# The normalised rows of layer 2 go out already split: one ACT copy less per tile, stores and loads of both parts in place of a plain copy

## The reference, cut to what matters

```python
x = layernorm(x + attn_1(x))                      # layer 1
# layer 2
a = attention(rmsnorm(x, ln1_w))                  # 16 heads of 32, causal
mod = 0.1 * tanh(a @ A)
h = rmsnorm(x, ln2_w)
gate = silu(h @ W_in.T + mod * (h @ A) @ B)
up = h @ W_up.T
x = layernorm(x + x + (gate * up) @ W_down.T)
```

## Time and profile before

| | before |
|---|---|
| time, median of 3 runs | 2830.97 us (2830.84 to 2834.05) |
| the profiled execution, its own time | 2830.6 us |
| its span in the profile | 2828.7 us |
| mean granted TensorE clock | 0.973 of full speed |
| busy: PE, DVE, ACT, POOL | 93%, 56%, 47%, 23% |
| SP's queue (q1): packets, MB, share of the 16 DMA engines | 170676, 260.57, 38.3% |

### The profile page before, as it was taken

How to read it: one execution, slowest core, us unless ns; L and a number is a source line. 1 busy time by engine, 2 the same in 40 slices (tenths; PEclk the granted TensorE clock), 3 DMA queues, 4 the chain that set the end, 5 groups by cost and what they waited for, 6 DMA issues and landing times.

```text
span 2828.7 us, 40920 instructions
## 1 busy us (share of the span) xinstructions
PE 2642.4 (93%) x13584; PEld 2020.4 (71%) x13584; DVE 1580.3 (56%) x4310; ACT 1334.4 (47%) x2755; POOL 645.5 (23%) x527
## 2 busy tenths in 40 slices
PE   5999999999768999999999989999999999999998
PEld 4777777777446666666666656888888888888886
DVE  4778777777635877787786775222222333333333
ACT  2777777777624666666666665111111321111111
POOL 5466655556321222212212211000000000000000
PEclk8999999999868999999999989999999999999999
DMA  5566656665535545546545544111111311111100
GB/s 137 103 149 144 137 124 140 145 147 132 132 98 130 121 102 136 120 105 134 119 107 132 114 103 143 64 55 46 46 46 47 102 58 47 46 46 46 46 30 30
DMA packets 173802, 276.44 MB, mean 98 GB/s; under 512 B 29108, under 2 KB 53428, under 8 KB 172980
## 3 DMA queue, kind: packets, MB, share of 16 engines
q1 hardware_dynamic: 170676, 260.57, 38.3%
q0 software_dynamic: 2304, 12.58, 1.3%
q10 hardware_dynamic: 640, 1.05, 0.1%
HBM read 97.03 MB, written 42.99 MB: 50 GB/s over the span
## 4 chain that ended last, share of the span: by engine, by line
PE 53%; DVE 7%; SPq 3%; issue 3%; ACT 3%; DMA 2%; POOL 0%; ACTq 0%; DVEq 0%; POOLq 0%
PE b_scores_ps L2428 13%; PE b_lin_ps L2417 13%; PE b_pv_ps L2398 6%; PE b_scores_t_ps L2398 6%; PE b_lin_ps L1955 5%; PE b_pv_ps L307 2%; DVE b_prob L290 2%; PE b_lin_ps L1918 2%; PE b_scores_t_ps L271 2%; DVE b_junk L202 1%; PE b_scores_ps L188 1%; DMA b_k_stack<-b_k_split 1%; SPq L258 1%; SPq L254 1%; PE b_lin_ps L2423 1%
## 5 line engine op out<-in xcount | busy, mean ns | idle before, releaser
L290 DVE TENSOR_TENSOR a_prob<-a_scores_t_ps,a_prob 128x384 fp32r<-128x384 f32 (+1 forms) x384 | 225.4, 593 | 135.0 <-ACT a_scores_t_ps L283 133.5
L282 ACT ACTIVATE b_prob<-b_scores_t_ps 128x384 fp32r<-128x384 f32 (+1 forms) x384 | 199.7, 520 | 212.5 <-PE b_scores_t_ps L273 191.3
L290 DVE TENSOR_TENSOR b_prob<-b_scores_t_ps,b_prob 128x384 fp32r<-128x384 f32 (+1 forms) x384 | 226.8, 594 | 118.1 <-ACT b_scores_t_ps L283 117.4
L307 PE MATMUL a_pv_ps<-a_prob,a_value 128*65 128x512 f32 (+3 forms) x1024 | 272.3, 334 | 0.5 <-DVE a_prob L290 0.5
L282 ACT ACTIVATE a_prob<-a_scores_t_ps 128x384 fp32r<-128x384 f32 (+1 forms) x384 | 201.9, 526 | 148.9 <-PE a_scores_t_ps L273 124.2
L307 PE MATMUL b_pv_ps<-b_prob,b_value 128*33 128x512 f32 (+3 forms) x1024 | 270.6, 333 | 0.1
L202 DVE CUSTOM_DVE_ANT_0 b_junk<-b_scores_ps,spare 128x512 bf16<-128x512 f32 (+3 forms) x512 | 226.9, 483 | 61.5 <-PE b_scores_ps L188 60.2
L202 DVE CUSTOM_DVE_ANT_0 a_junk<-a_scores_ps,spare 128x512 bf16<-128x512 f32 (+3 forms) x512 | 226.9, 483 | 34.4 <-PE a_scores_ps L188 32.2
L2365 DVE TENSOR_TENSOR b_res<-b_scores_ps,b_first_gate 128x512 f32<-128x512 f32 x64 | 44.2, 691 | 333.5 <-PE b_scores_ps L2428 333.5
L2365 DVE TENSOR_TENSOR stage<-b_scores_ps,b_junk 128x512 f32<-128x512 f32 x64 | 44.3, 692 | 329.0 <-PE b_scores_ps L2428 329.0
L990 PE MATMUL a_lin_ps<-x_split,w_split 128*128 128x512 f32 x768 | 215.5, 398 | 0.0
(11 more groups left out here) (298 smaller groups left out, 5874.3 us busy)
## 6 DMA issues: line engine op xcount, KB each, us to landing
a_q_stack<-a_q_split SPq DMA_DIRECT2D x192, 128.0 KB, 3.5
a_k_stack<-a_k_split SPq DMA_DIRECT2D x192, 128.0 KB, 3.6
b_q_stack<-b_q_split SPq DMA_DIRECT2D x192, 128.0 KB, 3.3
b_k_stack<-b_k_split SPq DMA_DIRECT2D x192, 128.0 KB, 3.7
spare<-h_t SPq DMA_DIRECT2D x16, 1024.0 KB, 6.2
stage<-in_x_t SPq DMA_DIRECT2D x8, 1024.0 KB, 6.7
a_sum_hi<-a_pv_raw SPq DMA_DIRECT2D x32, 256.0 KB, 3.8
spare<-a_pv_raw SPq DMA_DIRECT2D x32, 256.0 KB, 4.0
```

The lines of the kernel that those rows point to most:

```text
L282: act.activation(at.prob_hi[:, k % at.ring, 0:w], at.scores_t_ps[:, k % 2, 0:w], ACT.Exp, scale=SCALE)
L290: dve.tensor_tensor(at.prob_lo[:, k % at.ring, 0:w], at.scores_t_ps[:, k % 2, 0:w], at.prob_hi[:, k % at.ring, 0:w], ALU.subtract).then_in ...
L307: mm = pe.matmul(at.pv_ps[0:at.vcols, h % 2, kt * P:SEQ], at.value[:, kt, g * GH + h, :], prob[:, k % at.ring, col:col + width], start=(kt ...
```

## The change

The plain copy h_turn is gone. ACT makes only the high part of each tile; DVE takes the low part from the PSUM bank itself. The DRAM tensor h_t now holds both parts, 2 MB a batch in place of 1, and `store_h` stores them from h_split in two transfers of 1 MB once all four tiles are split; in step g=2 it now stands after spread_in instead of ahead of spread_out. The MLP loads both parts straight into its operand tiles (`load_h`, two transfers of 1 MB), and `input_hi` and `input_lo` are gone. As DVE now reads the bank, PE's transposes of tiles 2 and 3 wait for h_split_ready instead of h_hi, and the first projections for it too. The load for run 0 moves from step g=3 of the last batch to its step g=2, ahead of gather.

```diff
-            def store_h(b, t):
-                apart(sp, at.ones_set, h_copied, b * TT + t + 1)
-                sp.dma_start(h_hbm[:, :, bass.ds(b * SEQ + t * P, P)], h_turn[:, t, :, :]).then_inc(h_out, 16)
+            def store_h(b):
+                sp.wait_ge(h_split_ready, (b + 1) * TT)
+                for part in range(2):
+                    sp.dma_start(h_hbm[part, :, :, bass.ds(b * SEQ, SEQ)],
+                                 h_split[:, part, :, :].bitcast(F32)).then_inc(h_out, 16)
...
                     mlp.load_z(sp, mlp.start, 0)
-                if last and g == 3:
-                    sp.wait_ge(at.score_read, BATCH * GROUPS * UNITS)
                     mlp.load_h(sp, mlp.start, 0)
                 if not first:
                     gather(*group(b, g, -1))
-                if g == 2 and not last:
-                    for t in range(TT):
-                        store_h(b + 1, t)
                 if not first:
                     spread_out(*group(b, g, -1))
                 if g < 3 and not first:
                     spread_in(*group(b, g, -1))
+                if g == 2 and not last:
+                    store_h(b + 1)
                 if g == 2 and has(b, 2):
                     load(b + 2)
...
             def h_tile(b, t):
                 act.wait_ge(h_turned, b * TT + t + 1)
+                if t == 0:
+                    at_least(act, h_out, b * 32)
                 bank = lin_ps[:, t % 2, :].rearrange("p (c n) -> p c n", c=KC)
-                act.activation(h_turn[:, t, :, :], bank, ACT.Copy).then_inc(h_copied, 1)
                 act.activation(h_split[:, 0, :, t * P:t * P + P], bank, ACT.Copy).then_inc(h_hi, 1)
...
-                    if last and g == 3 and 5 <= slot < 5 + KC:
-                        mlp.input_hi(act, mlp.start, slot - 5)
...
             def h_tile(b, t):
                 dve.wait_ge(h_hi, b * TT + t + 1)
-                dve.tensor_tensor(h_split[:, 1, :, t * P:t * P + P], h_turn[:, t, :, :],
+                bank = lin_ps[:, t % 2, :].rearrange("p (c n) -> p c n", c=KC)
+                dve.tensor_tensor(h_split[:, 1, :, t * P:t * P + P], bank,
                                   h_split[:, 0, :, t * P:t * P + P], ALU.subtract).then_inc(h_split_ready, 1)
...
                 if t >= 2:
-                    pe.wait_ge(h_hi, b * TT + t - 1)
+                    pe.wait_ge(h_split_ready, b * TT + t - 1)
...
     def load_h(self, sp, run, second):
-        at_least(sp, self.h_ready, run.n * KC)
-        sp.dma_start(self.h_stage[:, :, :], self.h_hbm[:, :, self.rows_of(run.n, second)]).then_inc(self.h_in, 16)
+        at_least(sp, self.up_made, (run.n - 1) * FT)
+        for part in range(2):
+            sp.dma_start(self.h_split[run.pair][:, part, :, :].bitcast(F32),
+                         self.h_hbm[part, :, :, self.rows_of(run.n, second)]).then_inc(self.h_in[run.pair], 16)
...
                 if ft == 0:
-                    pe.wait_ge(self.h_ready, run.n * KC + KC)
+                    pe.wait_ge(self.h_in[run.pair], run.used * 32 + 32)
```

More of the change, by code:

```diff
@@ L1182, in gate_layer @@
         h_split = sb("h_split", [P, 2, KC, SEQ], F32R)
-        h_turn = wide[:, :, :].rearrange("p t (c n) -> p t c n", c=KC)
         a_stage = sb("a_stage", [P, KC, RANK])
@@ L1234, in gate_layer @@
         h_turned = sem("h_turned")
-        h_copied = sem("h_copied")
         h_hi = sem("h_hi")
@@ L1271, in load @@
                 apart(sp, at.ones_set, h_split_ready, b * TT)
-                apart(sp, at.ones_set, h_out, b * TT * 16)
                 apart(sp, at.ones_set, ab_ready, b * 2)
@@ L1341, in step @@
                     sp.wait_ge(x1_out, BATCH * 16)
-                    sp.wait_ge(h_out, BATCH * TT * 16)
+                    sp.wait_ge(h_out, BATCH * 32)
                     sp.wait_ge(o_made, BATCH * TT)
@@ L1385, in _ @@
             store_x1(0)
-            for t in range(TT):
-                store_h(0, t)
+            store_h(0)
             stack_send(sp, at, 0, 0, 0)
@@ L1476, in body @@
                         pool.wait_ge(x1_out, BATCH * 16)
-                        pool.wait_ge(h_out, BATCH * TT * 16)
                         pool.wait_ge(h_split_ready, BATCH * TT)
@@ L1823, in step @@
                         mlp.low_b_lo(dve)
-                    if last and g == 3 and 6 <= slot < 6 + KC:
-                        mlp.input_lo(dve, mlp.start, slot - 6)
                     if g == 2 and not last:
@@ L1941, in project @@
                             pe.wait_ge(h_hi, (b + 1) * TT)
+                            pe.wait_ge(h_split_ready, b * TT + 3 + i)
                         elif b == 0 and g == 1:
@@ L2140, in __init__ @@
         self.z_stack = [b_stack, low_stack]
-        self.h_stage = both.spare
         self.h_split = [both.x_split, h_split]
@@ L2153, in __init__ @@
         self.w_ready = sem("w_ready")
-        self.h_in = sem("h_in")
-        self.h_hi = sem("h_hi")
-        self.h_ready = sem("h_ready")
+        self.h_in = [sem(f"h_in{i}") for i in range(2)]
         self.z_in = [sem(f"z_in{i}") for i in range(2)]
@@ L2271, in low_b_hi @@
         act.activation(self.low_b_split[:, 0, :], self.low_b_stage, ACT.Copy).then_inc(self.b_hi, 1)
-    def input_hi(self, act, run, c):
-        if c == 0:
-            act.wait_ge(self.h_in, run.n * 16 + 16)
-            at_least(act, self.up_made, (run.n - 1) * FT)
-        act.activation(self.h_split[run.pair][:, 0, c, :], self.h_stage[:, c, :], ACT.Copy).then_inc(self.h_hi, 1)
     def activations(self, act, last_tanh, last_z):
@@ L2294, in body @@
                     last_z()
-                if 2 <= ft < 2 + KC and not run.is_(2 * BATCH - 1):
-                    self.input_hi(act, run.next(), ft - 2)
                 for k in self.weight_splits(run, ft):
@@ L2319, in low_b_lo @@
                           ALU.subtract).then_inc(self.b_ready, 1)
-    def input_lo(self, dve, run, c):
-        dve.wait_ge(self.h_hi, run.n * KC + c + 1)
-        dve.tensor_tensor(self.h_split[run.pair][:, 1, c, :], self.h_stage[:, c, :], self.h_split[run.pair][:, 0, c, :],
-                          ALU.subtract).then_inc(self.h_ready, 1)
     def add(self, dve, run, second):
@@ L2377, in body @@
                     self.normalise(dve, run.former())
-                if 2 <= ft < 2 + KC and not run.is_(2 * BATCH - 1):
-                    self.input_lo(dve, run.next(), ft - 2)
                 for k in self.weight_splits(run, ft):
@@ L2524, in build @@
     x1 = scratch("x1", [BATCH * SEQ, D])
-    h = scratch("h_t", [P, KC, BATCH * SEQ])
+    h = scratch("h_t", [2, P, KC, BATCH * SEQ])
     z = scratch("z", [2, RANK, BATCH * SEQ])
```

## The result

| | before, same chip | after |
|---|---|---|
| median | 2831.91 us (2830.84 to 2834.05, 4 runs) | 2855.30 us (2851.80 to 2857.51, 4 runs) |
| profiled execution: own time, span | 2830.6, 2828.7 us | 2856.64, 2854.7 us |
| mean granted clock | 0.973 | 0.970 |

The ratio is 1.0078, 95% interval 1.0065 to 1.0091: 23.4 us more, or 26.0 between the two profiled executions. The forecast was 2842, with a range of 2830 to 2851. The direction was right, the size was not.

The account below looks back on a forecast made before the run. TensorE alone was taken to bound the MLP, while PE, ACT, DVE and DMA take turns in layer 2's attention. Terms -0.5 + 9.6 - 0.4 + 4.6 - 1.3 = +12.0 on 2830.6 gave 2842 us, range 2830 to 2851.

Parts of the forecast that it names:

- Prologue, -0.5: Before layer 2's first projection: without ACT's plain copy the last transposed tile is ready earlier, 0.5 us saved.
- ACT and DVE in step g=2, -0.4 a batch: Batches 0 to 6: DVE's wait for ACT's copy shrinks and PE's new waits are covered, 0.4 us saved a batch.
- The queue in step g=2, +1.6 a batch: Batches 0 to 5: stores delay the stack pairs by 2.0 us, less 0.4 saved, so +1.6 a batch, +9.6 in all.
- Batch 6, -0.4: Batch 6 has no load behind the store, which fits into the gap, so it gains 0.4 us.
- Last batch, g=2, +4.6: Two 1 MB loads ahead of gather make its sums land 4.6 us later, with ACT and DVE standing.
- Last batch, g=3, -1.3: The four input splits go from the last batch's step g=3, saving 1.3 us.
- The MLP, 0: Fewer ACT and DVE operations are worth nothing and the extra load is hidden, since TensorE alone bounds it: 0 us.
- rival 1: Not slower: SP's queue has room and nothing lands later, 2815 to 2826 us; chance 0.12.
- rival 2: Partly absorbed: each delay counts by half, 2826 to 2836 us; chance 0.20.
- rival 3: Worse: SP itself is held behind the stores, or a longer low clock around the last step, 2851 us and above; chance 0.10.

Follow-up runs that it names:

- run 1: The changed kernel with both h stores moved from step g=2 to behind gather in step g=3: 2833.03 us, ratio 0.9996 to the kernel before.
- run 7: The changed kernel with the attention load issued ahead of the two h stores in step g=2, not behind them: 2843.34 us, ratio 1.0032 to before.
- run 6: The changed kernel with both h stores issued by GpSimd on its own queue, later in step g=2 than in the change: 2864.14 us, ratio 1.0114 to before.
- run 2: The changed kernel with the last batch's load of h for the MLP back in its step g=3: 2843.81 us, ratio 1.0041 to before.
- run 3: The changed kernel with h stores behind gather in step g=3 and the last batch's load back in step g=3: 2827.47 us, ratio 0.9971 to before.
- run 10: The changed kernel with h stores behind gather of the next batch's step g=1 and the last batch's load in step g=3: 2828.14 us, ratio 0.9982 to before.
- run 8: The changed kernel with both parts stored tile by tile (eight 256 KB transfers) at the old place ahead of spread_out: 2834.39 us, ratio 1.0005 to before.
- run 9: The changed kernel with both h stores at the end of step g=2, behind stack pair 1: 2873.98 us, ratio 1.0135 to before.
- run 11: The changed kernel with both h stores between stack pair 0 and the store of x1 in step g=2: 2877.34 us, ratio 1.0160 to before.

## Why the prediction was wrong, step by step

- **Prologue, -0.5.** Not to be seen: layer 2's first step starts at 889.1 in both, and at 887.1 to 895.1 in the other traces.
- **ACT and DVE in step g=2, -0.4 a batch.** Right: -0.5 in batch 6. DVE's wait before its low part fell from 4.6 to 1.3 us over 7 batches, its tile takes 0.67 us from PSUM (the mean of 32) where it took 0.69 from SBUF, and the new waits of PE, longer than forecast (6.7 us in 14), are covered.
- **The queue in step g=2, +1.6 a batch: this is the step that failed, by its size.** Steps g=2 and g=3 of batches 0 to 5 are 18.0 us longer than before, 3.0 a batch. The mechanism, pairs that land later behind the store and hold up what needs them, is there. Its term was 2.0 us of delay, as the store's 5.65 us less 3.1 to 3.9 us of room in the engines. Against run 1, which has no store at this place, pair 0 lands 3.9 us later (23.3 / 6) and pair 1, which was to be late by the same, 3.0 (18.2 / 6). So of the room that I counted only 1.75 us were used. The room by bytes priced the attention load at 371 GB/s; where it goes first, in run 7, the window moves 257. Why the rest wasn't used no run shows. The row that I named for the pairs went the other way (ACT's wait for b_k_stack 6.2 us and not near 20), while PE's wait for them rose.
- **What that step left out: the shift row.** It made steps g=2 13.5 us longer against run 1, 2.25 a batch, where the prediction had them shorter. I looked at what stands behind the stores on SP's queue and left out what the other queue carries through the same 16 engines, though it was PE's first need in the next step, landing 3.3 us after its issue with 1.6 us to spare. By the table above this moved the wait from one step to the other; a cost of its own isn't shown. Adding its 2.25 to the full delay of the pairs would count the same wait twice.
- **The sum, corrected:** 12.0 + 8.4 (batches 0 to 5: 18.0 in place of 9.6) + 0.6 (batch 6) + 1.8 and - 0.2 (the last batch) + 0.5 (prologue) = 23.1, against 23.4 measured. That it lies so near is luck in part: the terms are of two single executions, which are 26.0 apart, and the 2.9 that are left stand in other steps, most of it in step (7,1).

The Trainium skill, "DMA: Bandwidth & Descriptors", section "Issuing engines are not separate DMA queues", says that transfers of SP, ACT and GpSimd run on the same 16 engines; run 6 agrees (stores on a third queue, and shift row and pairs as late as in the change). Its section "Queues, rings and completion order" says that an engine takes turns between its queues packet by packet, from which I would expect 16 KB on a queue of its own to pass a full SP queue quickly; here they took 8.04 us.

- **Batch 6, -0.4.** Right for its step g=2, 25.8 against 26.3; its step g=3 was 0.7 longer, for which I know no reason.
- **Last batch, g=2, +4.6.** Right in kind, +6.4 in the trace, and 6.5 and 5.6 by moving the load alone (runs 2 and 3). The 371 GB/s of a store were too fast for these loads: from 1700 to 1709 us the engines moved 230 GB/s, with a share of 0.81. A lower clock stands there before too (0.57 from 1688 to 1700 us), but the change has it for longer (0.54 from 1709 to 1725); its price isn't known.
- **Last batch, g=3, -1.3.** Right: -1.5.
- **The MLP, 0.** Right: +0.03 us.
- **Rivals.** 1 and 2 are out with the store where the change has it. Of rival 3, which has 2851 and above, the hold of SP is not what came: three issues took up to 3.66 us, but the same three took 3.36 before, and the engines were full meanwhile. The lower clock, which I had put there, did come, in steps g=3 of inner batches too; its own price is open. In batch 1 it follows PE's wait for the shift row, and step (1,3) with 3.4 us of it took 25.96 us, the same step of run 7 without it 26.14. Step (5,3) with 6.8 us took 29.63 against 26.15, but there pair 1 was late as well (PE stood 2.5 us for it, against 0.8).
- **The +3.3 of step (7,1)** is not shown to be the change's: over the traces of the experiments that step varies from 27.8 to 32.1 us, 30.5 with the store late, 32.1 at the old place, 28.1 in run 10.

## What to carry to other kernels

When a transfer is moved, list every transfer that is under way in the same stretch, on all queues, and ask of each who waits for it; the smallest one, issued by another engine, may be the first that is missed. A wait that grows where one didn't expect it needn't be the cost: ask what the same work would have waited for next. And free time of the engines, counted from a mean share, is not yet room that a new transfer can use: here 3.1 to 3.9 us were counted and 1.75 used. Then look for a stretch in which the engines move nothing: the same 2 MB a batch cost next to nothing at three places of this kernel (runs 1, 8 and 10) and 10 to 44 us at five (the change and runs 6, 7, 9 and 11, against run 1). Work saved on engines that are busy half the time (here half of ACT's copies of h and all input splits of the MLP) brought 5 to 8 us of 2831 at best, less than one badly placed transfer took.

## What the runs showed of the hardware that was not expected

- A transfer of 16 KB on ACT's queue landed after 8.04 us with 3 MB under way on SP's. The same transfer took 3.3 us beside the 1 MB load alone, and 5.5 to 6.3 us beside the same 3 MB with the load ahead of the stores.
- Two orders of the same transfers, load then stores or stores then load, moved 310 and 301 GB/s over the same 19 us, and yet were 12 us of the kernel apart.
- The first of two megabytes cost 2.5 to 4.6 us in six batches, not clear of noise, the second 17.7 or more.
